# Zeroing three key buffers on VectorE, with their rows of ones written by DMA, in a planned transformer kernel

## The reference, cut to what matters

```python
x = x + LN(L0_attn(LN(x)))   # 6 layers: windowed attention, 16 heads of 8, residual + LN, GELU FFN, residual + LN
x = x + LN(L0_ffn(LN(x)))    # token-shift mixing with a gate
x = x + LN(L1_attn(LN(x)))   # causal attention with phase gates
x = x + LN(L1_ffn(LN(x)))    # router, top 3 of 8 experts, GELU FFN
# x is [4, 512, 128]
# L0_attn, per layer: keys = concat([past, x]); scores = q k^T / sqrt(8), valid where 0 <= q_pos - k_pos <= 125
# attn = softmax(scores); o = attn v; x = LN(x + o Wo + bo); x = LN(x + gelu(x W1 + b1) W2 + b2)
```

## Time and profile before

| | |
|---|---|
| median of 3 runs | 1080.01 us (1079.85 to 1083.88) |
| profiled execution | 1081.28 us |
| its span, first to last instruction | 1079.5 us |
| mean granted TensorE clock | 0.971 |
| busy: PE / DVE / ACT / POOL | 997.3 / 793.7 / 748.3 / 396.2 us |

### The profile page before, as it was taken

How to read it: one execution, slowest core, us unless ns; L and a number is a source line. 1 busy time by engine, 2 the same in 40 slices (tenths; PEclk the granted TensorE clock), 3 DMA queues, 4 the chain that set the end, 5 groups by cost and what they waited for, 6 DMA issues and landing times.

```text
span 1079.5 us, 47209 instructions
## 1 busy us (share of the span) xinstructions
PE 997.3 (92%) x20024; PEld 699.7 (65%) x20024; DVE 793.7 (74%) x2420; ACT 748.3 (69%) x1405; POOL 396.2 (37%) x528
## 2 busy tenths in 40 slices
PE   4799999999999999999999999999879789999995
PEld 2377677687777768777767767767656344455764
DVE  6886878768687877868778786868858999881321
ACT  6367666766776676677677666768784578899652
POOL 8312244333324433332344333234684444211212
PEclk9699999999999999999999999999988899999998
DMA  6740213041323303142231403220030121401220
GB/s 192 130 84 5 62 37 89 13 123 37 63 62 83 87 3 93 33 107 62 49 77 48 101 24 63 62 58 18 3 60 21 43 45 21 117 26 42 69 70 20
DMA packets 72626, 64.80 MB, mean 60 GB/s; under 512 B 16226, under 2 KB 66914, under 8 KB 72418
## 3 DMA queue, kind: packets, MB, share of 16 engines
q1 hardware_dynamic: 71554, 60.99, 23.6%
q10 hardware_dynamic: 864, 0.79, 0.5%
HBM read 15.70 MB, written 1.05 MB: 16 GB/s over the span
## 4 chain that ended last, share of the span: by engine, by line
PE 62%; ACT 17%; DVE 13%; issue 4%; POOL 3%; DMA 0%; ACTq 0%; POOLq 0%; DVEq 0%; SPq 0%
PE b L819 11%; PE b L720 8%; PE b L931 7%; PE b L800 5%; PE b L834 5%; ACT hid L1140 4%; PE b L753 4%; DVE mx L1267 4%; DVE mx L1270 3%; PE b L1003 3%; PE b L922 3%; ACT probs L1065 3%; PE b L993 3%; PE b L906 2%; ACT L1140 2%
## 5 line engine op out<-in xcount | busy, mean ns | idle before, releaser
L1065 ACT ACTIVATE probs<-b 128x443 f32<-128x443 f32 (+2 forms) x736 | 355.4, 547 | 131.8 <-PE b L800 78.3
L1270 DVE TENSOR_REDUCE mx<-b 128x2 f32<-128x378 f32 (+1 forms) x768 | 350.3, 510 | 94.2 <-PE b L753 93.3
L819 PE MATMUL b<-probs,vals 128*32 128x189 f32 (+5 forms) x3968 | 181.2, 311 | 4.2 <-ACT probs L1065 1.9
L720 PE MATMUL b<-band,identb 64*64 64x252 bf16 x2304 | 171.9, 287 | 14.2 <-DVE mx L1270 4.6
L819 PEld LDWEIGHTS b<-probs,vals 128*32 128x32 f32 x3968 | 111.2, 110 | 54.7 <-issue 13.0
L800 PE MATMUL b<-qpack,kpack 64*64 64x189 bf16 (+5 forms) x3968 | 137.7, 235 | 0.2 <-issue 0.2
L720 PEld LDWEIGHTS b<-band,identb 64*64 64x64 bf16 x2304 | 67.2, 105 | 92.0 <-DVE mx L1270 42.2
L753 PE MATMUL b<-kpack,qpack 62*64 62x189 bf16 (+1 forms) x3072 | 124.3, 240 | 0.0
L1594 POOL TENSOR_SCALAR veps<-mv 128x4 f32<-128x4 f32 x48 | 11.1, 230 | 297.1 <-DVE mv L1376 297.1
L931 PE MATMUL b<-w,hid 128*128 128x128 f32 x768 | 102.9, 282 | 0.5 <-DVE xres L1445 0.4
L1267 DVE TENSOR_REDUCE mx<-b 128x1 f32<-128x512 f32 (+7 forms) x256 | 96.5, 446 | 6.8 <-PE b L768 6.5
(11 more groups left out here) (175 smaller groups left out, 1690.9 us busy)
## 6 DMA issues: line engine op xcount, KB each, us to landing
qpack<-qparts SPq DMA_DIRECT2D x168, 128.0 KB, 3.5
kpack<-kparts SPq DMA_DIRECT2D x162, 128.2 KB
qpack<-mrows SPq DMA_DIRECT2D x224, 4.0 KB
w<-in_w SPq DMA_DIRECT2D x12, 256.0 KB, 3.9
w<-in_wa SPq DMA_DIRECT2D x12, 256.0 KB, 2.7
w<-in_wb SPq DMA_DIRECT2D x12, 256.0 KB, 2.9
rowt<-in_rowt SPq DMA_DIRECT2D x6, 384.0 KB, 3.4
stream<-in_x SPq DMA_DIRECT2D x4, 256.0 KB, 4.4
```

Source lines behind the costliest of these rows:

```text
L720: pe.matmul(out, identb[rows, rows], rhs.unsqueeze(1).to_broadcast([64, 2, 2, EDGE]), start=True, stop=False, skip_group_check=True)
L819: mm = pe.matmul(bank("sum", u, group)[32 * j:32 * j + 32, q0:q0 + w - skip], vals[:, u % 2, at:at + 32], probs[:, n % SETS, j, col + skip ...
L1065: act.activation(probs[:, n % SETS, j, 0:width], bank("exp", u, v, b)[:, 0:width], ACT.Exp, scale=SCALE).then_inc(a_emptied, 1)
L1270: red = dve.tensor_reduce(out[:, 2 * tb:2 * tb + 2], read[:, 0:2 * width].rearrange("p (t k) -> p t k", k=width), AX.X, ALU.max)
```

## The change

`kclean` becomes three VectorE memsets of zero. A new SP job `ones` waits for all three and issues two DMAs, each from a DRAM array of ones into two rows of all three buffers (27,648 bytes a row). `pack_first` waits for these DMAs instead of the first clean. The load of `max_row` and ScalarE's wait for it go. Planner costs are changed (blank, GELUs, `nroot`, expert landing, a new 95 ns for a freed bank where 50 stood), and all weights of the planner are new, so the order of every engine may differ.

```diff
-RESTART = 170
+FREED, RESTART = 95, 170
...
-TURN_WORTH = 172051
-TABLE_WORTH = 497529
-SLACK = {"act": 248, "dve": 0, "pe": 18, "pool": 23, "sp": 5575}
+TURN_WORTH = 238538
+TABLE_WORTH = 657425
+SLACK = {"act": 298, "dve": 0, "pe": 0, "pool": 133, "sp": 11734}
...
-                rooms.append((job.end + LEAD[e] + 50, self.room[k], k))
+                rooms.append((job.end + LEAD[e] + FREED, self.room[k], k))
...
-             else (which + "clean", u)], line=None if first else "pack", landing=3000)
+             else (which + "clean", u), ("ones",) if first else None], line=None if first else "pack", landing=3000)
...
-                add("act", ("gelu", u, f), 460, [("hid", u, f), ("ffn", u - 2, CHUNKS - 1) if u > 1 else None],
+                add("act", ("gelu", u, f), 570, [("hid", u, f), ("ffn", u - 2, CHUNKS - 1) if u > 1 else None],
...
-    add("pool", ("nroot", b, k), 1840, [("nstats", b, k)])
+    add("pool", ("nroot", b, k), 1950, [("nstats", b, k)])
...
-        add("sp", ("expert", b, r), 2400, [("chosen", b), used], line="expert", landing=3300)
+        add("sp", ("expert", b, r), 2400, [("chosen", b), used], line="expert", landing=2400)
...
-            add("act", ("egelu", b, r, f), 340,
+            add("act", ("egelu", b, r, f), 470,
...
-    for name, loads in ((("x", 0), 1), (("row",), 1), (("in",), 3), (("ident",), 1), (("x", 1), 1), (("load", 0), 7),
+    for name, loads in ((("x", 0), 1), (("in",), 3), (("ident",), 1), (("x", 1), 1), (("load", 0), 7),
...
-    add("dve", ("blank",), 2700)
+    add("sp", ("ones",), 500, [("kclean", BUFS - 1)], landing=4000)
+    add("dve", ("blank",), 3400)
...
-        add("act", ("kclean", n), 2050, [("row",)], line="kclean")
+        add("dve", ("kclean", n), 2050, line="kclean")
...
-                act.wait_ge(k_clean, 1)
+                act.wait_ge(ones_loaded, 32)
...
-            def clean_keys(buf):
-                act.activation(kpack[:, buf, :, :].rearrange("p v k -> p (v k)").bitcast(F32),
-                               zero[:, :].to_broadcast([P, PAIRS * KEYS // 2]), ACT.Identity, bias=max_row[:, 0:1]
-                               ).then_inc(k_clean, 1)
-
             act.wait_ge(zero_ready, 1)
-            act.wait_ge(row_loaded, 16)
...
+                elif kind == "kclean":
+                    dve.memset(kpack[:, where[0], :, :].rearrange("p v k -> p (v k)").bitcast(F32), 0.0).then_inc(k_clean, 1)
...
-                elif kind == "row":
-                    sp.dma_start(max_row[:, :], d["max_row"]).then_inc(row_loaded, 16)
+                elif kind == "ones":
+                    sp.wait_ge(k_clean, BUFS)
+                    for e in range(2):
+                        sp.dma_start(kpack[64 * e + BODY:64 * e + 64, :, :, :].rearrange("p b v k -> p (b v k)").bitcast(F32),
+                                     d["ones"]).then_inc(ones_loaded, 16)
...
-        "max_row": np.where(r >= BODY, twice, np.float32(0.0)).astype(np.float32),
+        "ones": np.full((64 - BODY, BUFS * PAIRS * KEYS // 2), twice, np.float32),
```

More of the change, by code:

```diff
@@ new lines @@
+TABLE_WORTH = 657425
+SLACK = {"act": 298, "dve": 0, "pe": 0, "pool": 133, "sp": 11734}
+BIAS = {"active": 581143, "add": -369212, "band": -100077, "blank": 94727, "bo": -379790, "bo_in": -143827, "cat":
+        533099, "cnorm": -23, "consts": 8559, "even": -112602, "exp": -2273475, "ffn": -1884851, "heads": 99752,
+        "hid": 1495988, "ident": 209102, "in": 278593, "k": -291213, "kclean": -433553, "later": 817801, "load":
+        331810, "lower": -227666, "masks": 770092, "max": 615943, "maxrows": 160502, "mrows": 194323, "norm":
+        1523183, "ocat": 877124, "odd": -849389, "ones": -14266, "out": 5272, "pack": -247088, "parts": -348612,
+        "place": 10110, "places": -459366, "q": 1118230, "qclean": -46601, "recip": 325777, "residue": 97681,
+        "rest": -8247, "root": 109892, "scale": -119286, "score": 1422637, "shifts": 111972, "sin": -431472,
+        "split": 100023, "stats": -76185, "sum": -54068, "top": -1824278, "turn": 1508356, "v": -379090, "weigh":
+        -7494587, "x": -1132445}
@@ new lines @@
+LATE = {"cat": 286115, "chosen": -57097, "cout": 409742, "eadd": -402281, "egelu": 74253, "ehid": -1045923, "eout":
+        -1046444, "exp": -286246, "expert": -48919, "gate": 604214, "gated": -678878, "gates": 9474, "heads":
+        -214726, "k": 2426254, "logits": 1061093, "max": 100798, "maxrows": -391333, "mix": -252663, "mixed":
+        -610273, "mixin": 346226, "mixv": -9141, "nadd": 24588, "nroot": 107514, "nscale": -590452, "nstats":
+        -413664, "open": -516066, "out": 721406, "parts": 443854, "phase": 308028, "q": 617507, "recip": 209705,
+        "rexp": -429612, "router": -35298, "rows": 2805238, "score": 698336, "scored": 67, "split": -967132,
+        "spread": -414379, "square": -279886, "state": 89889, "store": -381915, "sum": -118487, "take": -908003,
+        "tanh": 454802, "top": 3012683, "turn": -318091, "v": 19229, "weigh": 262025, "weight": -92181, "window":
+        -70829}
@@ L568, in whole_phase @@
         band, band_first = sb("band", [P, SPAN], BF16), sb("band_first", [P, 2, P + 1], BF16)
-        max_row, minus_half, zero = sb("max_row", [P, 1]), sb("minus_half", [P, 2 * TILES]), sb("zero", [P, 1])
+        minus_half, zero = sb("minus_half", [P, 2 * TILES]), sb("zero", [P, 1])
         gain, shift, bo = sb("gain", [P, P]), sb("shift", [P, P]), sb("bo", [P, P])
@@ L635, in whole_phase @@
         x_loaded = [sem(f"x_loaded{b}") for b in range(BATCH)]
-        row_loaded, in_loaded, ident_loaded = sem("row_loaded"), sem("in_loaded"), sem("ident_loaded")
+        ones_loaded, in_loaded, ident_loaded = sem("ones_loaded"), sem("in_loaded"), sem("ident_loaded")
         band_loaded, bo_loaded, later_loaded = sem("band_loaded"), sem("bo_loaded"), sem("later_loaded")
@@ L1232, in _ @@
                     expert_gelu(*where)
-                elif kind == "kclean":
-                    clean_keys(*where)
                 elif kind == "pack":
```

## The result

The changed kernel takes 1083.18 us, the median of 20 runs (1080.1 to 1085.52), against 1078.97 us for the kernel before in 20 runs beside it. The ratio is 1.0038, 95% interval 1.0029 to 1.0048: 0.4% or 4 us slower, where 1073.6 us were forecast.

What follows compares the result with a forecast made beforehand. TensorE was taken to fill the middle, leaving gains at the start and from 770 to 900 us; -0.9 + 0 - 2.6 - 2.9 = -6.4 us from a median of 1080.0 gave 1073.6 us, range 1063 to 1089.

Steps and rivals of the forecast that it cites:

- The bound: Whole run: TensorE fills the long middle, which no order can move much; gains lie at the start and 770 to 900 us.
- Part 1: Start, ScalarE: losing three cleans lets `nscale` of element 0 start 0.9 us earlier; -0.9 us taken for the start.
- Part 2: Start, VectorE: three memsets, 5.9 us together, fit into its 8.4 us of waiting before 21.5 us.
- The close call: Start, VectorE: a second clean may run just before `place` is ready, starting `place` 0.6 us later, otherwise 0.9 us earlier.
- The bound that I gave, +0.6 us: Start: the worst case taken, with `place` late and nothing recovered; the best case was -2.1 us.
- Part 3: Start, SP: the ones by DMA land by about 20.5 us, hidden before ScalarE's first key pack at 24.93; cost 0.
- Part 4: New order of all engines: 0 in the middle, -2.6 and -2.9 us late, bounds -9 and +9 us late.
- The 0 for the middle: Long middle: tables rank as before and TensorE is 97.6% used, so no change; bounds -4 and +4 us.
- -2.6 - 2.9 = -5.5 us: Late: two table loads gone, -2.6 us; an eighth of the 23.1 us TensorE idleness from 770 to 900 recovered, -2.9 us.
- The flip: ScalarE at 768.72 us: table switched inside a batch of four GELUs for one exponential; its removal saves two loads, 2.6 us.
- VectorE becomes the bound of the start: Rival, chance 0.08: cleans fall behind `place` of several elements or the maxima, adding 5.9 us to the path, 1085.9 us.
- a worse late part: Rival, chance 0.14: the late part is ordered worse, a third more idleness there, 7.7 us, giving 1087.7 us.

Runs made afterwards that it cites:

- the two repairs by hand: Changed kernel with early table load and second memset behind `place` 0: 1.0055 against before; changed kernel with `nscale` and `place` of elements 2 and 3 earlier: 1.0025.
- the third spliced kernel: New fill and order for jobs started before 60 us, then the old order: 1.0106 against the kernel before, median 1090.14 us.

## Why the prediction was wrong

**The bound.** Right for the long middle from about 200 us on, in which the changed kernel's delay moved by only 1 us from row 5 to row 22, and right that start and late part can be moved. It was wrong to begin the immovable middle at 60 us: the new order of the first units behind it loses 4 us.

**Part 1, -0.9 us for ScalarE's obstacle.** This term failed. It assumed that `nscale` 0 needs only its offset; in the trace of before ScalarE's first table load, 3.82 to 5.10 us, came with the first clean, directly behind the wait for `max_row` and long before the offset was there at 8.35. With the cleans gone nothing asks for the table earlier, and its 1.28 us came onto the path: `nscale` at 9.72. And the 0.9 us, where an experiment did get them, did not reach the maxima.

**Part 2, the memsets.** Their duration was right, 1.98 us against 1.97. Two sizes were wrong. VectorE waits 0.43 us more ahead of each (the changed kernel's waits put 1.3 us ahead of the three), so they take 7.2 us, not 5.9. And the idle 8.4 us of the earlier trace rows were counted as cover, though part of it lies between steps that depend on each other; pieces of 2 us put there pushed `rest` and the statistics. The close call fell on the bad side: the second memset ran ahead of `place` 0, as the greedy rule let me fear. What the fill costs depends on the order: 3.6 us in the old one, 3.0 in the old one up to 700 us, 0.5 in the old one up to 60 us with the new one behind it (all with the early table), 6.9 in the old one with the late table, and in the new one nothing, since the same order with the old fill is slower still (1.0062 against 1.0038). The bound that I gave, +0.6 us, was too low for the old order, but the fill is not what makes the changed kernel slower.

**Part 3, the ones.** As predicted, hidden: issued at 17.09, long before the first pack at 26.14, which waited for ScalarE's copy of values and not for them. The estimate from the Trainium skill (DMA: Bandwidth & Descriptors), 4.4 us for 55.3 KB on each of two engines, can be held against the trace's DMA packets. Four of them carry 27,648 bytes each, one row. They run two at a time, starting at 17.93, 18.28, 19.88 and 20.05 us, which fits the rule of two engines for two rows, and the last ends at 21.90, 4.8 us after the issue. The total is close by luck: the moving took 4.0 us where 1.9 were estimated, and only 0.8 us passed before it where 2.5 were counted.

**Part 4, the order.** This is the step that failed and decided the sign. I priced the new order at the late part and at 0 in the middle, and never for the start, where the earlier trace rows had 19.2 us of TensorE's idleness and a clock of 0.59 behind it. The order alone with the old fill is 6.7 us slower (1.0062), with 6.6 us of delay already there at row 3, 7.9 in the middle. Taken apart, the jobs up to 60 us with the new fill put +6.1 us into the middle, the new order behind them +4.3 by itself; the changed kernel has +8.8. The middle from 200 us on was about 0 as predicted.

The 0 for the middle also rested on a wrong reading of the tables. I wrote that they rank the same as before, having looked at `stats`, `add`, `top` and `exp` alone. But on VectorE `rest` stood 1.1 million below `add` (-270,774 against 844,360) and stands 0.36 million above it now (-8,247 against -369,212), on ScalarE `sum` fell from 2,368,721 to -54,068, and `exp` was not lowest by over a million before: `odd` stood at -708,579. No run tests which of these changes costs.

The late part had the right sign and about the right size, -2.6 - 2.9 = -5.5 us against 6.2 measured with the new late order alone. The size is luck in part: the 2.9 us were to come out of TensorE's idleness from 770 to 900, and that stayed at 130 - 106.37 = 23.6 us against 23.1. What was gained lies between rows 22 and 23 and between rows 25 and 27, and half of it is shorter busy time, which I had not priced. Its reasons were only half right. The flip is gone; ScalarE's timeline where the earlier trace rows stood, and the group of the earlier trace rows:

```profile
777.01 1.28 ACT L1141 ACT_TABLE_LOAD   x1
778.30 2.42 ACT L1141 ACTIVATE hid<-b,cols 128x512 f32<-128x512 f32 x4
780.74 1.28 ACT L1066 ACT_TABLE_LOAD   x1
```

```profile
L1141 ACT ACT_TABLE_LOAD x25 | 32.1, 1283 | 17.7 <-PE b L923 16.7
```

All four GELUs stand behind one load. But there are still 25 such loads, since another batch is cut in the changed kernel, the one at 198 us. All table loads together are 70 where they were 74, 5.1 us less of ScalarE: two more before 250 us, two fewer from 748 to 900, four fewer behind 900. That the truer costs would make the gain, as I argued, is not borne out: the costs alone from 700 us made the kernel 2.1% slower, the weights alone 1.2%, only both together are faster. But as such half-switched planners write orders of their own, this does not say which of the two made the late gain.

**The rivals.** "VectorE becomes the bound of the start", given 0.08 and 5.9 us, is nearest in its time, but not in its cause: without any memset the new order is as slow. Nothing in my list had a worse start from the order itself. That 1083.2 lies between 1063 and 1089 is no merit of the sum: the upper end came from a worse late part, and the late part got better.

What stays open: which jobs of the new start and of the first units' new interleaving make the loss (the two repairs by hand did not find them), and which single swap of the new late order gains most. The parts also don't add up exactly: 11.4 us for start and fill and -0.5 us for the rest make 10.9, and the changed kernel loses 4.2. In the middle of the traces they nearly do (6.1 + 4.3 against 8.8), so the rest of the gap arises late, where the third spliced kernel, the new start with the old late order, is 11.4 us slower by its median but only 4.4 us at row 27 of its fastest execution.

## What to carry to other kernels

Before taking an operation off an engine, look at what else it did there: the first use of a function table may pay for the load while the engine has nothing urgent to do, and the next instruction inherits it; a one-column activation up front brought back 3.3 us in one order and nothing in another. Idle time between dependent steps is not cover for a block of 2 us: ask which queued instruction stands behind it, and follow that one to the bound. When a plan is made anew, price each stretch by itself, the start above all, rank every job of an engine's table and not only the known ones, and compare written orders by splicing them: of five kernels whose planner changed tables on the way only one, with everything switched at 700 us, was of use. And before a busy sum is read as work done, look whether the same instructions took equally long.

## What the runs showed of the hardware that was not expected

A VectorE memset of 128x2304 started 0.42 to 0.43 us after the instruction ahead of it, with nothing to wait for, all three times in the changed kernel, and the six of the kernel with doubled memsets show 0.42 to 0.43 too; other VectorE instructions of the start that had nothing to wait for followed within 0.11 us, except the first large memset (0.50).

Small VectorE instructions can take many times as long beside GpSimd: COPY and TENSOR_SCALAR of 128x8 took 1.24 and 1.19 us in the kernel before, while GpSimd ran TENSOR_TENSOR of 128x512 (25.20 to 29.36 us), and 0.14 and 0.20 us in the changed kernel, where GpSimd ran none of that size beside them.

The granted clock of TensorE stood at its lower level (1.2 GHz) in one stretch of the start before, 37.4 to 57.9 us, and in two in the changed kernel, 28.0 to 41.7 and 51.9 to 62.2 us. Ahead of the first of these TensorE had been waiting for the key pack since 26.1 us. This is why the windows read 0.90 and 0.70 where the earlier trace rows has 1.00 and 0.59: they are shares of time at 2.4 and at 1.2 GHz.

A load of ScalarE's table of 1.28 us, moved off the path in the old order, gave back 3.3 us by the ratios and 4.2 us in the middle of the traces, more than its length, with intervals that leave room for its length alone; in the new order it gave back nothing.
